# Part buffers, load order and waits in the projection and attention stages of a twelve-sublayer decoder

## The chip, the cores and the metric

The kernel is one program on one core of a Trainium2 chip. The metric is the device time in microseconds (us) of one execution. The core has five engines with instruction streams of their own: PE (TensorE, matmuls), DVE (VectorE), ACT (ScalarE), POOL (GpSimd) and SP (SyncE, which issues most DMAs here). They meet through semaphores.

## The reference, cut to what matters

The reference is a decoder of four levels with three sublayers each (self attention, cross attention to a context of 1024 tokens, and a feed-forward layer), each followed by `x = layernorm(x + sublayer(x))`. Tokens are 4 x 512, channels 256, heads 16 of 16 channels. The parts that the change touches are the projections and the softmax attentions:

```python
q, k, v = x @ Wq.T + bq, y @ Wk.T + bk, y @ Wv.T + bv     # y is x, or the context (4, 1024, 256)
scores = jnp.einsum('bhqd,bhkd->bhqk', q, k) * scale
weights = jax.nn.softmax(scores, axis=-1)
out = jnp.einsum('bhqk,bhkd->bhqd', weights, v)
```

The last cross attention (`L3_xattn`) has no projections: q is x itself, k and v are the context, and a mask of (4, 1, 512, 1024) is added to the scores. The first self attention (`L0_attn`) runs on x and on three coarser samplings of x.

## The kernel before, in words

Twelve sublayers run one behind the other, each as a few stages. Every stage is a block with one instruction stream an engine and semaphores of its own, and the engines meet at its end. Two kinds of stage are changed.

**`project_stage`** (lines 89 to 236) makes q and k and stores them in DRAM as bfloat16 parts. A float32 value is split in three parts (high, middle, low) so that bf16 matmuls can work on it. A unit is a tile of 128 channels by 512 tokens. For a unit of kind `split`, PE multiplies into PSUM (L161), ACT evacuates with the bias to `full` (L194), DVE rounds it to the high part (L224, a CAST) and subtracts to get `rest` (L228), ACT rounds `rest` to the middle part (L172), POOL subtracts to get the low part (L235), and SP stores the parts (L133): two DMAs for a q unit (384 and 256 KB), one for a k unit (384 KB). For a unit of kind `given` (the masked attention alone), the source is in SBUF already: ACT makes the high part straight from it (L183), and DVE, ACT, POOL and SP go on as before. `full` and `rest` have two buffers each, `parts` has three, so a unit's high part waits until the store of the unit three before has landed. On ACT the middle part of a unit stands behind the first step of the unit after it. Units of kind `kept` (values) are evacuated by ACT (L186) behind the split units. There are 32 split units in the pyramid's stage (16 fine, 16 coarse, the coarse ones behind 16 value tiles), 24 in `l1x`, 16 in `l2a`, 16 in `l3a`, and 24 given units in `l3x`, where one DMA brings the whole context (4 MB, `late`, L123) before the first store.

**`attention_stage`** (lines 285 to 914) runs six times: `pyr_coarse`, `pyr_core`, `l1x_core`, `l2a_core`, `l3a_core` (causal) and `l3x_core` (masked). Each has 4 batches of 4 groups of 4 heads, 16 bodies in all. Body g of an engine works on the scores of group g, while the maxima of group g+2 are made between them. The stacks of q and k have four buffers (`RING`), so that SP loads group g+3 in body g. In a body:

- PE: the first scores of group g (L665; they wait for the row of maxima of group g, `row_in`) alternate with the first pass (L597) over group g+2, whose first chunk waits for that group's loads (`loaded`). Behind the first four pairs come the last weighing of group g-1 (L632, `pv_done`) and the transposition of the maxima of group g+1 (`turn`, L611).
- DVE takes the maxima of the first pass (L773, or L769 with the mask) and negates the transposed ones (L787, L790). POOL splits these in three parts (L852, L853, L855, `row_made`).
- SP waits for `pv_done` of group g-1, then loads the values of group g+1 where they come from DRAM (L476; the two pyramid stages), the q and k of group g+3 (L473, 8 DMAs, 9 in `l3a`), and then the row of maxima of group g+1 (L509, 3 DMAs of 4 KB), behind `row_made`:

```python
            def group(b, g):
                before = later(b, g, -1)
                if exists(*before):
                    sync.wait_ge(pv_done, at(*before, nkt, nkt + ahead_tiles))
                    ...
                        load_group(*later(b, g, RING - 1))
                if exists(*later(b, g, 1)):
                    row(*later(b, g, 1))
```

- At the end of the body SP takes its turn with the sums of the weights and their inverses (bodies 0, 1 and 3 of a batch), and in `l3x` with the masks of the next batch.

The 12 bodies from the second to the thirteenth load a group. Loads of `l1x_core` and `l3x_core` have 1024 keys, the others 512. In the masked stage PSUM banks are seeded with `mask_k` by ACT (L715) and DVE (L797, every fourth tile) before the scores are added, and the maxima are taken of scores plus `mask_q`.

## Time and profile before

| | |
|---|---|
| runs | 5061.88, 5063.81, 5067.03 us; median 5063.81 |
| profiled execution | 5061.2 us, span 5059.4 us |
| busy, share of the span | PE 83%, DVE 56%, ACT 47%, POOL 29% |
| mean granted TensorE clock | 0.889 of full |

The stages that the change touches, by the stretches of the trace (us from the span's start; clock as a share of 2.4 GHz):

| stage | stretch | PE busy | clock | DMA share |
|---|---|---|---|---|
| pyramid projections | 17.0 to 138.0 | 106.4 | 0.96 | 0.73 |
| `pyr_coarse` | 136 to 338 | 132.0 | 0.68 | 0.57 |
| `pyr_core` | 338 to 566 | 202.3 | 0.92 | 0.55 |
| `l1x` projections | 1446.0 to 1537.7 | 78.5 | 0.88 | 0.51 |
| `l1x_core` | 1537 to 1958 | 397.2 | 0.94 | 0.32 |
| `l2a` projections | 2318.0 to 2374.5 | 46.6 | 0.89 | 0.50 |
| `l2a_core` | 2374 to 2592 | 203.1 | 0.93 | 0.40 |
| `l3a` projections | 4020.0 to 4079.8 | 49.8 | 0.83 | 0.48 |
| `l3a_core` | 4079 to 4281 | 168.8 | 0.92 | 0.44 |
| `l3x` parts | 4317.5 to 4396.6 | 0 | 0.50 | 0.57 |
| `l3x_core` | 4396 to 4948 | 463.9 | 0.90 | 0.36 |

The profile is one execution. An engine's busy time counts its instructions but not its waits; in the timeline, the brackets behind an instruction give how long the engine stood idle before it and what released it. Since the stages run one behind the other, a microsecond that a stage ends sooner is one off the whole.

### The profile page before, as it was taken

What the parts mean: (1) busy time and instruction counts of PE and PEld (TensorE: products, weight loads), DVE (VectorE), ACT (ScalarE), POOL (GpSimd) and SP (SyncE); (2) the same over time, 40 slices, a digit from 0 to 9 for tenths busy, and PEclk for the clock granted to TensorE, in tenths of its full rate; (3) what the DMA queues carried; (4) which work ended last, traced back from release to release, by engine and by line L of the source; (5) the groups of instructions that cost most, each with busy time, mean ns of one, the idle gap of its engine ahead of it and who ended that gap; (6) DMA issues with size and microseconds to landing.
All of it is one profiled execution on the core that took longest, in us unless ns stands there. A gap on an engine that the chain in (4) does not pass through costs nothing. (4 is left out here: it accounts for less than half of the span.)

```text
span 5059.4 us, 69705 instructions
## 1 busy us (share of the span) xinstructions
PE 4179.5 (83%) x20292; PEld 1977.2 (39%) x20292; DVE 2848.1 (56%) x6426; ACT 2373.1 (47%) x4593; POOL 1483.3 (29%) x1306
## 2 busy tenths in 40 slices
PE   7669766689678996897969799999997988089986
PEld 5322355377443332573334233333335644012223
DVE  3448473501566884004860387878863265298866
ACT  4337431243233775232743354545541245269992
POOL 3111131212130111112220288778880223200111
PEclk9669987799887998897989899999997989579998
DMA  7656212354033332674323311211201144633421
GB/s 249 129 104 120 48 49 34 118 201 147 29 133 56 65 61 64 242 235 126 84 69 148 117 61 60 74 60 59 74 28 45 36 107 86 193 63 90 93 54 37
DMA packets 374291, 486.70 MB, mean 96 GB/s; under 512 B 84772, under 2 KB 288020, under 8 KB 360516
## 3 DMA queue, kind: packets, MB, share of 16 engines
q1 hardware_dynamic: 366528, 447.77, 31.9%
q0 software_dynamic: 6384, 32.61, 2.1%
q8 instruction: 137, 2.24, 0.2%
q10 hardware_dynamic: 1068, 2.66, 0.2%
q14 instruction: 174, 1.43, 0.1%
HBM read 325.07 MB, written 143.92 MB: 93 GB/s over the span
## 5 line engine op out<-in xcount | busy, mean ns | idle before, releaser
L1251 POOL TENSOR_TENSOR lc_totals<-lc_totals,lc_weights 128x1024 f32<-128x1024 f32 (+1 forms) x320 | 623.3, 1948 | 165.1 <-DVE lc_totals L1200 134.1
L1160 ACT ACTIVATE lc_weights<-ps 128x1024 f32<-128x1024 f32 x384 | 393.6, 1025 | 441.0 <-PE ps L1077 430.0
L1181 DVE TENSOR_REDUCE lc_part_max<-ps 128x2 f32<-128x1024 f32 x384 | 466.1, 1214 | 200.5 <-PE ps L1057 199.0
L1077 PE MATMUL ps<-lc_q,lc_k 64*128 64x512 f32 x1536 | 397.3, 596 | 0.0
L1087 PE MATMUL ps<-lc_weights,lc_v 128*64 128x512 f32 x1536 | 372.2, 605 | 0.0
L773 DVE TENSOR_REDUCE l1x_core_part_max<-ps 128x1 f32<-128x512 f32 x512 | 316.4, 681 | 72.5 <-PE ps L597 72.4
L769 DVE CUSTOM_DVE_ANT_0 l3x_core_unused<-ps,l3x_core_mask_q 128x512 f32<-128x512 f32 x512 | 330.7, 686 | 6.4 <-DVE l3x_core_row_max L777 4.9
L732 ACT ACTIVATE l3x_core_weights<-ps 128x512 f32<-128x512 f32 x512 | 327.5, 694 | 7.8 <-PE ps L665 7.3
L732 ACT ACTIVATE l1x_core_weights<-ps 128x512 f32<-128x512 f32 x512 | 266.1, 602 | 84.0 <-PE ps L665 83.8
L715 ACT ACTIVATE ps<-l3x_core_mask_k 128x512 f32<-128x512 f32 x384 | 270.4, 704 | 32.9 <-DMA l3x_core_mask_k<-in_mask_k 32.9
L597 PE MATMUL ps<-l3x_core_k,l3x_core_q 96*128 96x512 bf16 x512 | 214.7, 420 | 54.0 <-DVE l3x_core_part_max L769 38.9
L235 POOL TENSOR_TENSOR proj_parts<-proj_rest,proj_parts 128x512 bf16<-128x512 f32 x112 | 143.9, 1292 | 311.1 <-ACT proj_parts L172 310.7
L597 PE MATMUL ps<-l1x_core_k,l1x_core_q 96*128 96x512 bf16 x512 | 209.0, 411 | 15.7 <-DMA l1x_core_k<-k_parts 11.8
L665 PE MATMUL ps<-l3x_core_q,l3x_core_k 99*128 99x512 bf16 x512 | 198.1, 393 | 19.4 <-ACT ps L715 18.2
L665 PE MATMUL ps<-l1x_core_q,l1x_core_k 99*128 99x512 bf16 x512 | 191.7, 385 | 5.3 <-ACT l1x_core_weights L732 5.3
L1377 DVE SCALAR_TENSOR_TENSOR rn_z<-ps,rn_z 128x256 f32<-128x256 f32 x112 | 45.6, 415 | 258.7 <-PE ps L1348 190.3
L773 DVE TENSOR_REDUCE pyr_core_row_max<-ps 128x1 f32<-128x512 f32 x256 | 158.4, 679 | 53.9 <-PE ps L597 53.8
L1077 PEld LDWEIGHTS ps<-lc_q,lc_k 64*128 64x128 f32 x1536 | 148.0, 189 | 94.0 <-issue 64.9
L773 DVE TENSOR_REDUCE l2a_core_row_max<-ps 128x1 f32<-128x512 f32 x256 | 158.5, 679 | 36.6 <-PE ps L597 36.5
L1057 PE MATMUL ps<-lc_k_round,lc_q_round 64*128 64x512 bf16 x768 | 151.9, 392 | 32.2 <-DVE lc_part_max L1181 20.8
L1087 PEld LDWEIGHTS ps<-lc_weights,lc_v 128*64 128x64 f32 x1536 | 93.3, 136 | 211.1 <-issue 119.4
L732 ACT ACTIVATE pyr_core_weights<-ps 128x512 f32<-128x512 f32 x256 | 133.3, 603 | 77.5 <-PE ps L665 77.4
(477 smaller groups left out, 8558.9 us busy)
## 6 DMA issues: line engine op xcount, KB each, us to landing
cf_w<-in_L1f_w SPq DMA_DIRECT2D x32, 1024.0 KB, 7.2
lc_k<-latent_k SPq DMA_DIRECT2D x32, 768.0 KB, 6.6
lc_v<-latent_values SPq DMA_DIRECT2D x32, 768.0 KB, 5.1
k_parts<-proj_parts SPq DMA_DIRECT2D x56, 384.0 KB, 2.8
latent_k<-feed_staged SPq DMA_DIRECT2D x64, 256.0 KB, 2.3
latent_values<-feed_staged SPq DMA_DIRECT2D x64, 256.0 KB, 2.0
q_parts<-proj_parts SPq DMA_DIRECT2D x40, 384.0 KB, 2.9
q_parts<-proj_parts SPq DMA_DIRECT2D x40, 256.0 KB, 3.0
```

The source lines that it names most:

```text
L597: mm = nc.tensor.matmul(out, q_stack[r][0:rows_a, j, qs], k_stack[r][0:rows_a, j, keys], start=True, stop=not causal)
L665: mm = nc.tensor.matmul(out, k_stack[r][0:rows_b, j, ks], q_stack[r][0:rows_b, j, qs], start=not seeded, stop=not (causal or seeded), skip ...
L715: nc.scalar.activation(k.ps[:, B0 + (g * NS + s) % B_BANKS, 0:nq], seed, ACT.Copy).then_inc(filled, 1)
L732: nc.scalar.activation(weights[:, (g * NS + s) % WEIGHTS, qs], k.ps[:, B0 + (g * NS + s) % B_BANKS, qs], ACT.Exp, scale=scale).then_inc(ex ...
L769: nc.vector.tensor_tensor_reduce(unused[:, n % 2, :], scores, mask_q[:, qi, keys], 1.0, -3.0e38, ALU.add, ALU.max, out).then_inc(a_taken, 1)
L773: nc.vector.reduce_max(out, scores, AX).then_inc(a_taken, 1)
L1057: mm = nc.tensor.matmul(k.ps[:, A0 + j, :], q_round[strip(j), g % 2, qs], k_round[strip(j), g % 2, keys], start=True, stop=True)
L1077: mm = nc.tensor.matmul(out[j], k_tile[g % RING][strip(j), i * P:(i + 1) * P], q_tile[g % RING][strip(j), :], start=False, stop=True)
L1087: mm = nc.tensor.matmul(k.ps[strip(j), ACC, 0:nq], v_tile[g % V_RING][:, i, strip(j)], weights[:, i % TILES, j, :], start=i == 0, stop=i = ...
L1160: nc.scalar.activation(weights[:, i % TILES, :, :], k.ps[:, B0 + (i % 2) * HEADS:B0 + (i % 2 + 1) * HEADS, 0:nq], ACT.Exp, scale=scale).th ...
L1181: nc.vector.reduce_max(own, k.ps[:, A0:A0 + HEADS, :], AX).then_inc(a_taken, 1)
L1251: nc.gpsimd.tensor_tensor(total, total, own, ALU.add).then_inc(added_by_pool, 1)
```

## The change

It has five parts.

1. `project_stage` gets six buffers of parts (`RING = 6`) in place of three.
2. In the masked attention's stage the context comes in eight pieces of 512 tokens (`pieces`), two ahead and one behind each of the first six stores; each given unit waits for its own piece.
3. In `attention_stage` SP sends the row of maxima of group g+1 first in the body, and waits for `pv_done` and issues the loads after it.
4. PE waits for the rows of ones (`set_up`) at the first group's scores and no longer before the first pass, except in the causal stage.
5. At the start of `l3x_core`, SP loads `mask_q` between the first and the second group, and DVE takes the maxima of group 0 and negates them ahead of its first fill.

```diff
-    VALUES = 6
+    VALUES, RING = 6, 6
+    PIECES_AHEAD = 2
...
-        stored_by.append((stored_by[i - 3] if i >= 3 else 0) + 16 * len(units[n][4]))
+        stored_by.append((stored_by[i - RING] if i >= RING else 0) + 16 * len(units[n][4]))
...
-        nc.sbuf_tensor(f"proj_parts_{k.stages}", [P, 3, 3, BANK], BF16) as parts,
+        nc.sbuf_tensor(f"proj_parts_{k.stages}", [P, RING, 3, BANK], BF16) as parts,
...
+            def load_piece(p):
+                if p < len(pieces):
+                    sync.dma_start(pieces[p][0], pieces[p][1]).then_inc(piece_in[p], 16)
+
+            for p in range(PIECES_AHEAD):
+                load_piece(p)
...
-                    for destination, taken in part_stores(unit[4], parts[:, i % 3, :, 0:unit[2]]):
-                        sync.dma_start(destination, taken).then_inc(parts_stored[i % 3], 16)
+                    for destination, taken in part_stores(unit[4], parts[:, i % RING, :, 0:unit[2]]):
+                        sync.dma_start(destination, taken).then_inc(parts_stored[i % RING], 16)
+                    load_piece(PIECES_AHEAD + i)
...
-                    if late and n == late_unit:
-                        act.wait_ge(late_in, 16 * len(late))
-                    if i >= 3:
-                        act.wait_ge(parts_stored[i % 3], stored_by[i - 3])
+                    for p, (_, _, first_unit) in enumerate(pieces):
+                        if first_unit == n:
+                            act.wait_ge(piece_in[p], 16)
+                    if i >= RING:
+                        act.wait_ge(parts_stored[i % RING], stored_by[i - RING])
...
-            for g in range(2):
-                load_group(0, g)
-            if by_batch:
-                load_batch_values(0)
+            load_group(0, 0)
             if mask is not None:
                 for qi in range(nqt):
                     load_mask_q(0, qi)
+            load_group(0, 1)
+            if by_batch:
+                load_batch_values(0)
...
             def group(b, g):
                 before = later(b, g, -1)
+                if exists(*later(b, g, 1)):
+                    row(*later(b, g, 1))
                 if exists(*before):
                     sync.wait_ge(pv_done, at(*before, nkt, nkt + ahead_tiles))
                     if exists(*later(b, g, 1)) and not kept:
                         load_values(*later(b, g, 1))
                     if exists(*later(b, g, RING - 1)):
                         load_group(*later(b, g, RING - 1))
-                if exists(*later(b, g, 1)):
-                    row(*later(b, g, 1))
...
-            if small:
+            if causal:
                 pe.wait_ge(set_up, 16 * n_ones)
...
+                if small and not causal and first(b, g):
+                    pe.wait_ge(set_up, 16 * n_ones)
...
+            maxima(0, 0, range(NCH))
+            negate(0, 0)
             if by_vector:
                 dve.wait_ge(opened, B_BANKS)
                 for s in range(LEAD):
                     if s in by_vector:
                         fill(0, 0, s, 1)
-            maxima(0, 0, range(NCH))
-            negate(0, 0)
             maxima(0, 1, range(NCH))
```

How the instructions move, at three places. On SP in `l2a_core`, from the last initial load on (`q_parts` and `k_parts` are loads of a group, `max_parts` a row of maxima), it stood before as:

```order
L473 DMA l2a_core_k<-k_parts 16x4x512 x3
L509 DMA l2a_core_q<-l2a_core_max_parts 1x16x128 x6
L473 DMA l2a_core_q<-q_parts 48x4x512
L473 DMA l2a_core_q<-q_parts 16x4x512 x3
L473 DMA l2a_core_k<-k_parts 48x4x512
L473 DMA l2a_core_k<-k_parts 16x4x512 x3
L509 DMA l2a_core_q<-l2a_core_max_parts 1x16x128 x3
```

and with the change:

```order
L483 DMA l2a_core_k<-k_parts 16x4x512 x3
L519 DMA l2a_core_q<-l2a_core_max_parts 1x16x128 x9
L483 DMA l2a_core_q<-q_parts 48x4x512
L483 DMA l2a_core_q<-q_parts 16x4x512 x3
L483 DMA l2a_core_k<-k_parts 48x4x512
L483 DMA l2a_core_k<-k_parts 16x4x512 x3
L519 DMA l2a_core_q<-l2a_core_max_parts 1x16x128 x3
```

Two rows (groups 0 and 1) stood ahead of the first load of the loop, and now three do: the row of group 2 is sent before group 4 is loaded. It is the same in all six attention stages.

On SP at the start of `l3x_core`, before:

```order
L473 DMA l3x_core_k<-k_parts 16x4x1024 x3
L473 DMA l3x_core_q<-q_parts 48x4x512
L473 DMA l3x_core_q<-q_parts 16x4x512 x3
L473 DMA l3x_core_k<-k_parts 48x4x1024
L473 DMA l3x_core_k<-k_parts 16x4x1024 x3
L487 DMA l3x_core_batch_values<-in_ctx 128x2048
L480 DMA l3x_core_mask_q<-in_mask_q 128x1024 x4
```

and with the change:

```order
L483 DMA l3x_core_k<-k_parts 16x4x1024 x3
L490 DMA l3x_core_mask_q<-in_mask_q 128x1024 x4
L483 DMA l3x_core_q<-q_parts 48x4x512
L483 DMA l3x_core_q<-q_parts 16x4x512 x3
L483 DMA l3x_core_k<-k_parts 48x4x1024
L483 DMA l3x_core_k<-k_parts 16x4x1024 x3
L497 DMA l3x_core_batch_values<-in_ctx 128x2048
```

The four loads of `mask_q` passed those of the second group and of the values. On DVE, the first fill of a bank (COPY) stood at the head of the stage and now stands behind the 32 chunks of group 0:

```order
L781 ISA l3x_core_unused,l3x_core_part_max<-ps,l3x_core_mask_q 128x512
L781 ISA l3x_core_part_max 128x1
L789 TENSOR_REDUCE l3x_core_row_max<-l3x_core_part_max 128x16
L799 TENSOR_SCALAR l3x_core_max_parts<-ps 16x128
L802 TENSOR_SCALAR l3x_core_negative<-ps 16x128
L809 COPY ps<-l3x_core_mask_k 128x512
L780 MEMSET l3x_core_held_back 1x1
```

So the first maxima no longer stand behind a fill that waits for `mask_k`.

## Rows read from the trace of the kernel before

**Rows 1.** Tile view, one stretch a stage: op, count, duration ns, first and last start

```profile
L611 PE MATMUL ps<-ident,pyr_coarse_row_max x13: 277/382/383, 170.8 to 314.3; 128*16 128x128 f32 x13
...
L611 PE MATMUL ps<-ident,pyr_core_row_max x13: 277/278/278, 385.4 to 535.1; 128*16 128x128 f32 x13
...
L611 PE MATMUL ps<-ident,l2a_core_row_max x13: 277/277/278, 2419.5 to 2560.4; 128*16 128x128 f32 x13
...
L611 PE MATMUL ps<-ident,l3a_core_row_max x13: 276/277/383, 4116.0 to 4254.1; 128*16 128x128 f32 x13
```

**Rows 2.** Waits of `pyr_coarse`: us in total, times, longest

```profile
PE ps L665 <- DMA pyr_coarse_q<-pyr_coarse_max_parts: 53.0, 14, 5.5
```

**Rows 3.** Timeline, PE: first-pass chunk and turn in `pyr_coarse`, `l2a_core`, `l3a_core`

```profile
179.71 0.40 PE L597 MATMUL ps<-pyr_coarse_k,pyr_coarse_q 96*128 96x256 bf16 x1
...
181.90 0.38 PE L611 MATMUL ps<-ident,pyr_coarse_row_max 128*16 128x128 f32 x1
...
2428.50 0.39 PE L597 MATMUL ps<-l2a_core_k,l2a_core_q 96*128 96x512 bf16 x1
...
2431.13 0.28 PE L611 MATMUL ps<-ident,l2a_core_row_max 128*16 128x128 f32 x1
...
4124.46 0.23 PE L597 MATMUL ps<-l3a_core_k,l3a_core_q 99*128 99x128 bf16 x1
...
4126.21 0.28 PE L611 MATMUL ps<-ident,l3a_core_row_max 128*16 128x128 f32 x1
```

**Rows 4.** Timeline, POOL and SP in the body of `l2a_core` that turns at 2419.47

```profile
2421.22 0.42 POOL L855 TENSOR_TENSOR l2a_core_max_parts<-l2a_core_negative,l2a_core_max_parts 16x128 bf16<-16x128 f32 x1
...
2419.59 1.74 SPq L473 DMA_DIRECT2D l2a_core_q<-q_parts  x4
...
2423.28 1.77 SPq L509 DMA_DIRECT2D l2a_core_q<-l2a_core_max_parts  x3
```

**Rows 5.** DMA view, 40 slices of 0.25 us from 171.36, 397.94 and 2419.59

```profile
GB/s 0 0 70 121 195 281 354 377 365 164 148 144 148 172 115 164 164 172 209 176 131 135 127 177 85 51 3 0 0 0 0 0 0 0 0 0 0 0 0 0
...
GB/s 295 262 229 197 262 164 197 37 133 186 227 254 305 307 262 168 152 160 139 152 172 148 160 168 209 197 160 139 139 165 101 33 5 0 0 0 0 0 0 0
...
GB/s 0 0 0 25 139 270 307 234 90 111 164 209 164 246 279 209 221 119 139 130 72 39 14 0 16 1 0 0 0 0 0 0 0 0 0 0 0 0 0 0
```

**Rows 6.** Tile view of `proj_rest`: pyramid's fine units, `l1x`, `l2a`, `l3a`

```profile
L228 DVE TENSOR_TENSOR proj_rest<-proj_full,proj_parts x16: 691/693/1471, 28.1 to 64.7; 128x512 f32<-128x512 f32 x16
...
L228 DVE TENSOR_TENSOR proj_rest<-proj_full,proj_parts x24: 691/693/1471, 1456.2 to 1513.5; 128x512 f32<-128x512 f32 x24
...
L228 DVE TENSOR_TENSOR proj_rest<-proj_full,proj_parts x16: 691/693/1460, 2327.9 to 2364.3; 128x512 f32<-128x512 f32 x16
...
L228 DVE TENSOR_TENSOR proj_rest<-proj_full,proj_parts x16: 691/693/1457, 4029.6 to 4068.7; 128x512 f32<-128x512 f32 x16
```

**Rows 7.** Timeline, DVE and POOL in the `l1x` projections

```profile
1499.80 0.42 DVE L224 CAST proj_parts<-proj_full 128x512 bf16<-128x512 f32 x1
...
1502.41 1.45 DVE L228 TENSOR_TENSOR proj_rest<-proj_full,proj_parts 128x512 f32<-128x512 f32 x1
1505.02 1.03 DVE L224 CAST proj_parts<-proj_full 128x512 bf16<-128x512 f32 x1 [1.15 <-DMA k_parts<-proj_parts]
...
1500.62 2.70 POOL L235 TENSOR_TENSOR proj_parts<-proj_rest,proj_parts 128x512 bf16<-128x512 f32 x2 [1.82 <-ACT proj_parts L172]
```

**Rows 8.** Tile view of `proj_rest`, `l3x` parts

```profile
L172 ACT ACTIVATE proj_parts<-proj_rest x24: 612/613/629, 4318.9 to 4391.1; 128x512 bf16<-128x512 f32 x24
```

**Rows 9.** Stretch view, `l3x` parts: stretch, length, busy PE, PEld, DVE, ACT, POOL, clock, DMA, GB/s

```profile
4317.50:4334.00 16.50, 0.00 (x0) 0.00 (x0) 2.92 (x3) 3.16 (x6) 2.27 (x2) 0.50 0.91 344
```

**Rows 10.** Timeline at the start of `l3x_core`, PE and DVE

```profile
4408.52 1.86 PE L643 MATMUL ps<-l3x_core_q,l3x_core_k 96*128 96x512 bf16 x4 [91.67 <-DMA l3x_core_k<-k_parts]
...
4425.21 0.69 DVE L769 CUSTOM_DVE_ANT_0 l3x_core_unused<-ps,l3x_core_mask_q 128x512 f32<-128x512 f32 x1
```

**Rows 11.** Tile view of `l2a_core_max_parts`: from a row's issue to its landing

```profile
DMA to landing us min/median/max: 1.6/2.1/4.2
```

More of the change, by code:

```diff
@@ L86, in _, with project_stage @@
                 act.dma_start(tile, source).then_inc(loaded, 16)
-def project_stage(k, units, weights, stores=(), late=(), late_unit=0, prefetch=()):
+def project_stage(k, units, weights, stores=(), late=(), late_unit=0, prefetch=(), pieces=()):
     nc = k.nc
@@ L107, in project_stage @@
         nc.sbuf_tensor(f"proj_rest_{k.stages}", [P, 2, BANK], F32) as rest,
-        nc.sbuf_tensor(f"proj_parts_{k.stages}", [P, 3, 3, BANK], BF16) as parts,
+        nc.sbuf_tensor(f"proj_parts_{k.stages}", [P, RING, 3, BANK], BF16) as parts,
         nc.sbuf_tensor(f"proj_value_{k.stages}", [P, VALUES, H, QUAD] if staged else [P, 1, 1, 1], F32) as value,
-        k.stage("weights", "late", "prefetched", "ready", "evacuated", "high", "remainder", "middle", "low", "ones", "parts_stored0",
-                "parts_stored1", "parts_stored2", "others_stored", *(f"value_stored{i}" for i in range(VALUES))) as (
-            weights_in, late_in, prefetched, ready, evacuated, high, remainder, middle, low, ones_set, *stored),
+        k.stage("weights", "late", "prefetched", "ready", "evacuated", "high", "remainder", "middle", "low", "ones",
+                "others_stored", *(f"parts_stored{i}" for i in range(RING)), *(f"value_stored{i}" for i in range(VALUES)),
+                *(f"piece{i}" for i in range(len(pieces)))) as (
+            weights_in, late_in, prefetched, ready, evacuated, high, remainder, middle, low, ones_set, others_stored, *more),
         nc.Block() as block,
     ):
-        parts_stored, others_stored, value_stored = stored[0:3], stored[3], stored[4:]
+        parts_stored, value_stored, piece_in = more[0:RING], more[RING:RING + VALUES], more[RING + VALUES:]
         @block.sync
@@ L141, in _ @@
                 sync.wait_ge(prefetched, 16 * len(prefetch))
-            for r in range(min(3, i)):
-                sync.wait_ge(parts_stored[(i - 1 - r) % 3], stored_by[i - 1 - r])
+            for r in range(min(RING, i)):
+                sync.wait_ge(parts_stored[(i - 1 - r) % RING], stored_by[i - 1 - r])
             if stores:
@@ L171, in take_middle @@
                 act.wait_ge(remainder, i + 1)
-                nc.scalar.activation(parts[:, i % 3, 1, 0:width], rest[:, i % 2, 0:width], ACT.Copy).then_inc(middle, 1)
+                nc.scalar.activation(parts[:, i % RING, 1, 0:width], rest[:, i % 2, 0:width], ACT.Copy).then_inc(middle, 1)
             i = j = 0
@@ L178, in _ @@
                 if unit[0] == "given":
[L179 to L183 removed]
+                    for p, (_, _, first_unit) in enumerate(pieces):
[3 more added lines that the diff above has]
+                        act.wait_ge(parts_stored[i % RING], stored_by[i - RING])
+                    nc.scalar.activation(parts[:, i % RING, 0, 0:unit[2]], unit[1], ACT.Copy).then_inc(high, 1)
                     i += 1
@@ L2738, in masked_attention @@
             project_stage(k, as_is(k.xT, q_parts) + as_is(ctxT, k_parts), [],
-                          late=[(ctxT[:], inp["ctxT"])], late_unit=T // BANK * CH,
+                          pieces=[(ctxT[:, :, t * BANK:(t + 1) * BANK], inp["ctxT"][:, :, t * BANK:(t + 1) * BANK], T // BANK * CH + t * CH)
+                                  for t in range(TC // BANK)],
                           prefetch=[(ow[:], inp["L3x_out_w"]), (ob[:], inp["L3x_out_b"].partition_broadcast(P))])
```

13 lines of the change are left out of this document (6 added, 7 removed).

## The prediction

> **What bounds the kernel now.** I read the stretch view first (its times are in the table above), because the stages stand one behind the other and each must be costed alone. Then the tile view for the pace of the loops, the timeline and the waits for what sets that pace, and the DMA view for when a transfer is through. PE is 83% busy over the span, but the stages that change have other limits. In the four attention stages with 512 keys a body lasts 11.5 to 12.5 us: between the first and the last of 13 turns lie 12 bodies, all of which load a group, so 143.5 / 12 = 11.96 us in `pyr_coarse`, 149.7 / 12 = 12.48 in `pyr_core`, 140.9 / 12 = 11.74 in `l2a_core` and 138.1 / 12 = 11.51 in `l3a_core` [rows 1]. In `pyr_coarse` PE stands 53.0 us waiting for rows of maxima, 14 times [rows 2]; in `l2a_core` it runs through. The split units of the projections follow each other every 2.4 to 2.6 us (57.3 / 23 = 2.49 in `l1x`; 2.44, 2.43 and 2.61 in the others) [rows 6]. The reader is to see there that DVE and POOL take turns: a subtraction of 0.69 us takes 1.45 while POOL's two run, and ends 0.54 us after they do (1502.41 + 1.45 = 1503.86; 1500.62 + 2.70 = 1503.32) [rows 7].
>
> **The row of maxima ahead of the loads.** This is the large term, and I take it for a loss. Body g of SP issues the loads of group g+3, and PE's first pass over that group begins in body g+1, behind the first score. So loads are due about one body after they are issued, as a row is. I follow `l2a_core` from one turn to the next.
> Before: the turn is at 2419.5 [rows 1]. SP issues the loads at once, 2419.59, and is at the row at 2423.28, so 8 loads take 3.7 us to issue and the row 1.77 [rows 4]. Bytes move until slice 22 of the DMA view, 5.5 us after the first issue [rows 5]; a completion comes behind. The pass begins at 2428.50, on loads that have been there for two us, and the next turn is at 2431.13, 2.6 us later [rows 3].
> Now: SP first waits for POOL's last split, which ends at 2421.22 + 0.42 = 2421.64, 2.2 us after the turn [rows 4], issues the row (0.1 + 1.8 us), and then the loads. How long they take from first issue to landing has no row; the bytes are through after 5.5 us in `l2a_core`, and after 6.75 and 8.25 in `pyr_coarse` and `pyr_core`, which load the same sizes [rows 5]. I take 6.5 for `l2a_core` (one us for the completion) and 7.5 for the other two, the middle of their slices; the ends are a us either way. Then the pass waits for the landing, and 2.6 us later comes the turn:
>
> - `l2a_core`: 2.2 + 0.1 + 1.8 + 6.5 + 2.6 = 13.2 us a body, 1.5 more than 11.74: 17.5 us over 12.
> - `pyr_coarse`: its values are issued ahead of the loads (0.45, a quarter of the 1.74 of four loads [rows 4]), and pass to turn takes 181.90 - 179.71 = 2.2 [rows 3]: 2.3 + 1.8 + 0.45 + 7.5 + 2.2 = 14.25, 2.3 more: 27.5 us.
> - `pyr_core`: the same with 2.6, 14.65, 2.2 more: 26 us.
> - `l3a_core`: 9 loads, so 6.8; pass to turn 4126.21 - 4124.46 = 1.75 [rows 3]: 2.3 + 1.8 + 6.8 + 1.75 = 12.65, 1.15 more: 13.7 us.
>
> Sum: **+85 us**, with a us of landing either way +40 to +130. The rows come early and their waits [rows 2] go, but what is late next is the load, by more. SP's own extra turns (sums, inverses, dense copies) stand behind both and fit in the longer body. In `l1x_core` and `l3x_core` a body lasts over 20 us, so a load that is 4 us later is still early: 0.
>
> **Six sets of parts, split units.** The store that a unit waits for is three units further back, so DVE's wait for it (1.15 us before the CAST at 1505.02 [rows 7]) goes. What is next is the turn-taking: CAST 0.42, subtraction 0.69 [rows 7], POOL 1.16 (half of 2.70, less the block at its start), 0.1 between, less 0.15 for each start that is hidden while blocked: 2.05 us a unit. That leaves 23 x 0.44 = 10 us in `l1x`, 15 x 0.38 = 6 in `l2a`, 15 x 0.56 = 8 in `l3a`, 15 x 0.39 = 6 in the pyramid's fine units [rows 6]. A us less each in `l1x`, `l3a` and the pyramid, where the first unit comes slowly from a cold PE or loads fill the queues: 9 + 6 + 7 + 5 = **-27 us**. The value tiles behind are PE's and start that much sooner; the pyramid's coarse units are PE's and only shift. Ends: 0, if the pace is already that of DVE and POOL, and -35.
>
> **The `l3x` parts**, buffers and pieces together. Given units follow every (4391.1 - 4318.9) / 23 = 3.1 us [rows 8]; the middle part of a unit stands on ACT behind the next unit's wait for a store. With six buffers the turn-taking allows 0.69 + 1.16 less 0.3, 1.6 us, 24 units in 38 us. DMA has more to do: 4.2 MB of context, 0.4 of weights, 8 x 0.65 of q and 16 x 0.39 of k are 16.1 MB, at 344 GB/s [rows 9] 47 us. With 3 us at the start and 4 behind the last store: 55 in place of 79.1, **-24 us**; ends -15 and -30. I let the pieces hold no unit up, since a piece is asked for behind each store and the first is needed by unit 8 only.
>
> **The start of `l3x_core`.** PE has group 0 at 4408.52, and DVE begins its maxima at 4425.21, behind a fill that waits for `mask_k` [rows 10]. With `mask_q` right behind group 0, its first quarter (0.5 MB, 1.5 us at 344 GB/s [rows 9]) is there at about 4410, and the fill (0.7) comes later: **-14 us**; ends 0 (the mask lands no sooner) and -16. The first scores wait for DVE's two rounds of maxima, so the gain goes through.
>
> **Rows of ones awaited later**: PE waits for the k loads at the starts, not for these [rows 10], so 0 in five stages and unchanged in the causal one; the loads are the cover, and without them it would be a us at most.
>
> **Sum.** 85 - 27 - 24 - 14 = +20 us on the profiled execution's 5061.2 (span 5059.4, 1.8 around it), which stands 2.6 below the median: 5063.8 + 20 = **5084 us**.
>
> **The rivals.**
> (a) *Loads in time, faster.* A row's DMA lands 2.1 us after its issue [rows 11]; if the last of eight loads did as much, they would be there 3.7 + 2.1 = 5.8 us after the first issue. With the sums above, the bodies would be 12.55, 12.95, 12.5 and 11.65 us (`pyr_coarse`, `pyr_core`, `l2a_core`, `l3a_core`), 0.6, 0.45, 0.75 and 0.15 over today: +23, so 5063.8 + 23 - 65 = 5022 us. It speaks against it that bytes still move after 5.5 to 8.25 us [rows 5]. The sign turns where landings come some 0.4 us sooner than my values (0.4 x 48 bodies = 19). The Trainium skill ("DMA: Bandwidth & Descriptors", "Anatomy of one DMA") has each DMA at some 2.0 us plus its bytes at 436 GB/s. By that rule 0.77 MB would take 3.8 us, a little more than the issues take. By that rule this rival would hold; the DMA view shows 100 to 300 GB/s instead [rows 5]. Chance 0.15.
> (b) *Never late.* PE would be through before SP, and the waits for rows go too: -65 - 53 [rows 2], 4946 us. It needs landings within 5 us. 0.03.
> (c) *The clock falls.* Stalls of 2 to 3 us in every body make PE run at 1.2 GHz, as in `pyr_coarse`, where the transposition takes 382 ns and not 277 [rows 1]. Then pass to turn doubles in `pyr_core` (+2.6 x 12 = 31) and `l3a_core` (+1.75 x 12 = 21): 5136 us. For it: one transposition of `l3a_core` at 383 [rows 1]; against: `pyr_core` has gaps today and all its 13 turns take 277 or 278 ns. 0.12.
> (d) *Six buffers buy nothing for split units*, as DVE and POOL set the pace: 5084 + 27 = 5111 us. 0.1.
>
> **How the numbers follow.** My forecast has 0.6, the rivals 0.4. The range is 5040 to 5135: it holds the forecast with its landings some 0.8 us off, (d) and the edge of (c), and leaves out (a) and (b). About 0.2% (10 us) is what a measurement of this kernel can tell from no change. Faster: (a), (b) and a tail of the forecast, 0.2. Same: the part of the forecast with +/-10 us, 0.14. Slower: 0.66.
>
> **What would show it.** Right: turns 13 to 15 us apart in the four short stages; PE's waits at first-pass chunks for `q_parts` or `k_parts`, none for rows of maxima; `l3x` parts near 55 us; DVE's first maxima of `l3x_core` some 14 us after its loads begin; split units every 2.05 us. Wrong: bodies of 12 us or less with PE waiting for nothing (a), transpositions at 382 ns in `pyr_core` (c), split units at 2.4 (d).

## The result, and the profile after

| | before | after |
|---|---|---|
| median | 5065.17 us (4 runs, 5061.88 to 5067.03) | 5127.95 us (4 runs, 5120.47 to 5131.85) |
| ratio, 95% interval | | 1.0117 [1.0105, 1.0130] |
| profiled span | 5059.4 us | 5130.1 us |
| mean granted clock | 0.889 | 0.883 |

The changed kernel is 63 us slower. The forecast had been 5084, in a range of 5040 to 5135: the direction and the mechanism are as forecast, and the loss is three times the forecast one. By its number alone the result is nearer to rival (c), the falling clock, at 5136.

Where it went, from PE's first and last instruction of each stage in the two profiled executions ("parts" is what lies between the stages, their only changed piece being the projections):

| stretch | before | after | difference | forecast |
|---|---|---|---|---|
| start to `pyr_coarse` (pyramid parts) | 146.1 | 136.3 | -9.8 | -5 |
| `pyr_coarse` | 190.7 | 222.3 | +31.6 | +27.5 |
| `pyr_core` | 217.6 | 264.6 | +47.0 | +26 |
| to `l1x_core` (parts) | 983.6 | 971.9 | -11.7 | -9 |
| `l1x_core` | 407.8 | 408.8 | +1.0 | 0 |
| to `l2a_core` (parts) | 425.5 | 422.1 | -3.4 | -6 |
| `l2a_core` | 208.4 | 239.3 | +30.9 | +17.5 |
| to `l3a_core` (parts) | 1498.4 | 1489.5 | -8.9 | -7 |
| `l3a_core` | 190.6 | 216.8 | +26.2 | +13.7 |
| to `l3x_core` (parts) | 129.1 | 107.7 | -21.4 | -24 |
| `l3x_core` | 538.6 | 526.1 | -12.5 | -14 |

The four short stages lost 135.7 us where 85 were forecast; all the other rows together gained 66.7 where 65 were forecast (the space between the two pyramid stages grew by 1.2). So the whole miss lies in one term.

**The pace.** The turns of the four short stages in the kernel after, as in [rows 1]:

```profile
L621 PE MATMUL ps<-ident,pyr_coarse_row_max x13: 278/382/383, 160.2 to 335.7; 128*16 128x128 f32 x13
...
L621 PE MATMUL ps<-ident,pyr_core_row_max x13: 277/382/383, 408.0 to 604.7; 128*16 128x128 f32 x13
...
L621 PE MATMUL ps<-ident,l2a_core_row_max x13: 277/278/383, 2474.3 to 2647.2; 128*16 128x128 f32 x13
...
L621 PE MATMUL ps<-ident,l3a_core_row_max x13: 277/382/383, 4193.6 to 4357.8; 128*16 128x128 f32 x13
```

A body now lasts 175.5 / 12 = 14.62, 16.39, 14.41 and 13.68 us. The median of a turn has gone from 278 to 382 ns in `pyr_core` and from 277 to 382 in `l3a_core`: more than half of them stand in stretches at the lower clock, which before was so in `pyr_coarse` only.

**What PE waits for.** Waits of PE in the kernel after (us in total, times, longest), in place of [rows 2]:

```profile
PE ps L607 <- DMA pyr_coarse_k<-k_coarse: 85.5, 13, 12.2
...
PE ps L607 <- DMA pyr_core_k<-k_parts: 51.0, 13, 12.0
...
PE ps L607 <- DMA l3a_core_k<-in_slopes: 29.6, 12, 3.5
PE ps L607 <- DMA l2a_core_k<-k_parts: 29.4, 13, 8.1
...
PE ps L677 <- DMA pyr_coarse_q<-pyr_coarse_max_parts: 9.5, 6, 4.8
```

L607 is the first pass (L597 before). Each of its waits comes once in a body that loads, and once at a stage's start (the longest, 8 to 12 us; `l3a`'s start is booked under the rows of ones). The rows of maxima, 53 us of waits in `pyr_coarse` before, are down to 9.5. One late transfer has been traded for another one, as the prediction says.

**One body.** The timeline of SP, POOL and PE in the body of `l2a_core` that turns at 2474.29, against [rows 3, 4]:

```profile
2474.29 0.28 PE L621 MATMUL ps<-ident,l2a_core_row_max 128*16 128x128 f32 x1
...
2476.05 0.42 POOL L867 TENSOR_TENSOR l2a_core_max_parts<-l2a_core_negative,l2a_core_max_parts 16x128 bf16<-16x128 f32 x1
...
2476.49 1.77 SPq L519 DMA_DIRECT2D l2a_core_q<-l2a_core_max_parts  x3
...
2478.30 2.00 SPq L483 DMA_DIRECT2D l2a_core_q<-q_parts  x4
...
2480.35 1.85 SPq L483 DMA_DIRECT2D l2a_core_k<-k_parts  x4
...
2484.96 0.39 PE L607 MATMUL ps<-l2a_core_k,l2a_core_q 96*128 96x512 bf16 x1 [1.63 <-DMA l2a_core_k<-k_parts]
...
2487.58 0.28 PE L621 MATMUL ps<-ident,l2a_core_row_max 128*16 128x128 f32 x1
```

Turn to row 2.2, row 1.8, first load to pass 6.66, pass to turn 2.62: 13.29 us, where the prediction had 13.2 by the same steps. This is a body at the high clock. The other kind, in `pyr_core`:

```profile
425.61 0.28 PE L621 MATMUL ps<-ident,pyr_core_row_max 128*16 128x128 f32 x1
...
427.99 1.78 SPq L519 DMA_DIRECT2D pyr_core_q<-pyr_core_max_parts  x3
...
430.45 1.92 SPq L483 DMA_DIRECT2D pyr_core_q<-q_parts  x4
...
437.88 0.39 PE L607 MATMUL ps<-pyr_core_k,pyr_core_q 96*128 96x512 bf16 x1 [3.24 <-DMA pyr_core_k<-k_parts]
...
438.10 0.38 PE L677 MATMUL ps<-pyr_core_q,pyr_core_k 99*128 99x512 bf16 x1
...
439.03 0.63 PE L677 MATMUL ps<-pyr_core_q,pyr_core_k 99*128 99x512 bf16 x1
...
440.02 1.94 PE L642 MATMUL ps<-pyr_core_weights,pyr_core_v 128*32 128x512 f32 x8
...
441.89 0.38 PE L621 MATMUL ps<-ident,pyr_core_row_max 128*16 128x128 f32 x1
```

The first chunk follows a wait of 3.24 us and still takes 0.39. From 439.03 on the same matmuls take 0.63 and the weighing 1.94 (1.06 ahead of the wait), and pass to turn is 4.01 us, not 2.6. The clock falls behind the gap, over the very stretch that everything then waits for. The stretch view (columns as in [rows 9]) has the granted clock at 1.00 up to 438, through the wait, and then at:

```profile
438.00:440.00 2.00, 2.00 (x7) 0.61 (x6) 1.70 (x3) 1.38 (x3) 0.00 (x0) 0.73 0.04 8
440.00:442.00 2.00, 2.00 (x10) 0.32 (x10) 0.82 (x2) 0.30 (x1) 0.00 (x0) 0.50 0.00 0
```

The body before this one has the same: a wait of 4.09 us, and matmuls of 0.63 us from 0.8 us behind it on. Not every wait has it: behind two of the twelve in `pyr_core`, of 2.70 and 2.79 us, pass to turn stays at 2.62.

**The parts.** The tile view of `proj_rest` after (pyramid's fine units, `l1x`, `l2a`, `l3a`, and the middle parts of `l3x`), against [rows 6, 8]:

```profile
L238 DVE TENSOR_TENSOR proj_rest<-proj_full,proj_parts x16: 691/694/1457, 27.9 to 56.9; 128x512 f32<-128x512 f32 x16
...
L238 DVE TENSOR_TENSOR proj_rest<-proj_full,proj_parts x24: 691/694/1457, 1526.7 to 1573.5; 128x512 f32<-128x512 f32 x24
...
L238 DVE TENSOR_TENSOR proj_rest<-proj_full,proj_parts x16: 691/694/1459, 2390.4 to 2421.2; 128x512 f32<-128x512 f32 x16
...
L238 DVE TENSOR_TENSOR proj_rest<-proj_full,proj_parts x16: 692/694/1457, 4117.6 to 4148.4; 128x512 f32<-128x512 f32 x16
...
L181 ACT ACTIVATE proj_parts<-proj_rest x24: 612/614/631, 4426.0 to 4473.8; 128x512 bf16<-128x512 f32 x24
```

The split units come every 1.93, 2.03, 2.05 and 2.05 us (46.8 / 23 = 2.03), where 2.05 was forecast from the turns that DVE and POOL take. The given units of `l3x` come every 47.8 / 23 = 2.08 us, down from 3.1. That is a mean of two paces. At both ends of the stage they come every 1.8 us, and between 4437.5 and 4452.7 every 3.05. There the DMA engines are full (share 1.07), and ACT waits for a store ahead of each of seven units, 12.0 us in all:

```profile
4440.00:4450.00 10.00, 0.00 (x0) 0.00 (x0) 2.42 (x4) 4.32 (x8) 3.62 (x3) 0.50 1.07 393
...
4442.94 0.63 ACT L193 ACTIVATE proj_parts<-l3x_ctxT 128x512 bf16<-128x512 f32 x1 [2.00 <-DMA q_parts<-proj_parts]
```

**The start of `l3x_core`.** PE's first matmul and DVE's first maximum, against [rows 10]:

```profile
4491.36 1.89 PE L653 MATMUL ps<-l3x_core_q,l3x_core_k 96*128 96x512 bf16 x4 [67.50 <-DMA l3x_core_k<-k_parts]
...
4493.88 0.69 DVE L781 CUSTOM_DVE_ANT_0 l3x_core_unused<-ps,l3x_core_mask_q 128x512 f32<-128x512 f32 x1
```

2.5 us from one to the other in place of 16.7 (4425.21 - 4408.52), 14.2 less. The first load of the stage is issued at 4479.46, so the maxima begin 14.4 us behind it, as the prediction has it.

### The profile page after: what moved, and what is told of

The parts are those of the page before. It is cut to its first block and busy times, and to the rows that moved or that the text cites. A ratio compares the mean times of both kernels' runs of the same rounds, so it can differ in the third digit from the quotient of the medians.

```text
span 5130.1 us, 69704 instructions
## 1 busy us (share of the span) xinstructions
PE 4215.5 (82%) x20292; PEld 1981.6 (39%) x20292; DVE 2872.0 (56%) x6426; ACT 2380.2 (46%) x4593; POOL 1491.2 (29%) x1306
## 5 line engine op out<-in xcount | busy, mean ns | idle before, releaser
L607 PE MATMUL ps<-l3x_core_k,l3x_core_q 96*128 96x512 bf16 x512 | 215.5, 422 | 39.7 <-DVE l3x_core_part_max L781 25.1
L607 PE MATMUL ps<-l1x_core_k,l1x_core_q 96*128 96x512 bf16 x512 | 209.6, 412 | 15.7 <-DMA l1x_core_k<-k_parts 11.8
L1389 DVE SCALAR_TENSOR_TENSOR rn_z<-ps,rn_z 128x256 f32<-128x256 f32 x112 | 45.9, 417 | 261.1 <-PE ps L1360 236.9
L744 ACT ACTIVATE pyr_core_weights<-ps 128x512 f32<-128x512 f32 x256 | 135.7, 602 | 111.8 <-PE ps L677 111.3
```

The costliest lines, as they stand in the source:

```text
L607: mm = nc.tensor.matmul(out, q_stack[r][0:rows_a, j, qs], k_stack[r][0:rows_a, j, keys], start=True, stop=not causal)
L744: nc.scalar.activation(weights[:, (g * NS + s) % WEIGHTS, qs], k.ps[:, B0 + (g * NS + s) % B_BANKS, qs], ACT.Exp, scale=scale).then_inc(ex ...
```

## The experiments

Each has its own runs of the kernel before on the same chip; ratios are to those. L-numbers of the changed kernel hold for the experiments made from it, moved by up to six lines where one adds lines.

### Undo the order on SP

```diff
                 before = later(b, g, -1)
-                if exists(*later(b, g, 1)):
-                    row(*later(b, g, 1))
                 if exists(*before):
...
                         load_group(*later(b, g, RING - 1))
+                if exists(*later(b, g, 1)):
+                    row(*later(b, g, 1))
```

> The change with the old order on SP (loads of a group, then the row of maxima); the other four parts stay. Theory (the order alone makes the loss): outside the four short stages the changed kernel is 65 us ahead of the one before, and inside them it lost some 136 us of its span; with the old order the four stages are back at bodies of 11.5 to 12.5 us and the time is 5065 - 65 = 5000 us, ratio 0.987. Rival (the loss comes from the stores or loads that now crowd the queues, or from the later wait for the rows of ones): the bodies stay near 14 to 16 us and the time stays above 5060.

Measured: 4991.33 us, ratio 0.9857 [0.9840, 0.9873]. The four stages last 188.8, 220.2, 210.1 and 187.9 us, within 3 us of before the change, and every other stretch stays within 4 us of the kernel after. Its turns in `pyr_core` and `l3a_core`:

```profile
L621 PE MATMUL ps<-ident,pyr_core_row_max x13: 277/278/383, 373.8 to 526.6; 128*16 128x128 f32 x13
...
L621 PE MATMUL ps<-ident,l3a_core_row_max x13: 277/278/382, 4084.3 to 4220.8; 128*16 128x128 f32 x13
```

12.73 and 11.38 us a body, at the higher clock again but for one turn in each. The order alone makes the loss: 5128 - 4991 = 137 us (132 by the ratios).

### The order on SP alone

The kernel before, with the same few lines moved the other way.

> The kernel before with only the new order on SP. Theory: the four short stages lose what they lost in the changed kernel, 136 us in the span of one execution, and nothing else moves: 5065 + 128 (the medians' +63, and 65 that the other parts gave) = 5190 to 5200 us, ratio 1.025; l1x_core and l3x_core within 2 us of before. Rival (the new order hurts only together with the other parts): under 5100.

Measured: 5202.67 us, ratio 1.0269 [1.0247, 1.0290], 3 us above what was expected. PE's waits are those of the kernel after:

```profile
PE ps L597 <- DMA pyr_coarse_k<-k_coarse: 86.2, 13, 12.7
...
PE ps L597 <- DMA pyr_core_k<-k_parts: 50.0, 13, 11.4
...
PE ps L597 <- DMA l3a_core_k<-in_slopes: 32.8, 12, 3.8
```

`l1x_core` lasts 407.8 us and `l3x_core` 538.1, as before. So the edit costs 139 us on the kernel before (5202.67 - 5064.15, its own runs of before; 136 by the ratio) and 137 us on the change, and the two sides add up: +137 to +139 for the order, -73 for the rest (4991.33 - 5064.15), +63 for both.

### Three and four sets of parts

Both with the loads first, as in the first experiment.

```diff
-    VALUES, RING = 6, 6
+    VALUES, RING = 6, 3
```

> The change with the old order on SP and three sets of parts instead of six; pieces and the rest stay. Theory (the wait for the store of three units before was the pace): split units go back from 2.05 us to 2.4 to 2.6 us each, and the l3x parts from 58 us to some 75: 27 + 15 more than the same kernel with six sets, 5040 us. Rival (the pieces alone mend the l3x parts): l3x parts near 60 us, 5027.

Measured: 5048.91 us, ratio 0.9968 [0.9958, 0.9978], so the three sets more are worth 58 us (5048.91 - 4991.33) of the 73, more than the 42 expected. By stretches of the profiled executions it is 8.4 us in the pyramid (136.5 to 144.9 until `pyr_coarse`), 14 in `l1x`, 6 in `l2a`, 2 in `l3a` and 20 in `l3x`, 50 in all; the profiled execution with three sets was the fastest of its nine, 9 us below their median. Here the units of `l1x` and the middle parts of `l3x` come every 2.53 and 2.93 us:

```profile
L238 DVE TENSOR_TENSOR proj_rest<-proj_full,proj_parts x24: 691/693/1469, 1458.6 to 1516.8; 128x512 f32<-128x512 f32 x24
...
L181 ACT ACTIVATE proj_parts<-proj_rest x24: 612/613/630, 4316.1 to 4383.5; 128x512 bf16<-128x512 f32 x24
```

> The change with the old order on SP and four sets of parts, between the three of before and the six of the change. Theory (the store of three units before was late by little: with three sets a unit took 2.5 us in place of 2.05, so it asks for 3 x 0.45 = 1.4 us more of room, and one set more gives 2.05): split units every 2.05 to 2.1 us, the time within 5 us of six sets, 4991 to 4996. Rival (the stores' own time sets the pace in stretches, and each set more takes a third of the loss away): 5010 to 5030.

With `RING = 4` in that line, measured: 4990.11 us, ratio 0.9870 [0.9853, 0.9888], the same as with six. In `l1x` the pace is that of six sets, in `l3x` it is 51.0 / 23 = 2.22 us, where the first experiment has 46.9 / 23 = 2.04:

```profile
L238 DVE TENSOR_TENSOR proj_rest<-proj_full,proj_parts x24: 691/694/1459, 1447.6 to 1494.5; 128x512 f32<-128x512 f32 x24
...
L181 ACT ACTIVATE proj_parts<-proj_rest x24: 613/615/632, 4279.2 to 4330.2; 128x512 bf16<-128x512 f32 x24
```

One set more does nearly all of it. The store was late by less than one unit.

### The context in one piece

With the loads first and six sets; the `pieces` list has one entry, the whole of `ctxT`, awaited by the first unit of the context.

```diff
-                          pieces=[(ctxT[:, :, t * BANK:(t + 1) * BANK], inp["ctxT"][:, :, t * BANK:(t + 1) * BANK], T // BANK * CH + t * CH)
-                                  for t in range(TC // BANK)],
+                          pieces=[(ctxT[:], inp["ctxT"], T // BANK * CH)],
```

> The change with the old order on SP and the whole context in one DMA of 4 MB at the start, six sets of parts. Theory (DMA volume bounds the l3x parts, and the pieces only spread it): the first stores wait behind the 4 MB, and the stage takes 3 to 8 us longer than with pieces; 5000 to 5008 us. Rival (the pieces were the main gain there): the stage is back at 70 to 79 us, 5015 or more.

Measured: 4989.75 us, ratio 0.9852 [0.9836, 0.9869], with 4991 for pieces: nothing. The middle parts take 45.9 us here, and 46.9 in the first experiment:

```profile
L181 ACT ACTIVATE proj_parts<-proj_rest x24: 612/613/630, 4295.1 to 4341.0; 128x512 bf16<-128x512 f32 x24
```

The stage and what surrounds it is 107.5 us against 106.6. The expected 3 to 8 us of loss are a miss. Both kernels have the DMA engines full for 25 to 30 us of the stage (share 0.96 to 1.08), so it may be that the bytes must be moved either way and their order makes no difference; beyond this pair no run shows it.

### The old start of `l3x_core`

With the loads first; `mask_q` goes behind group 1 and the values, and DVE's fill ahead of the maxima of group 0, as before.

> The change with the old order on SP, and l3x_core started as before (mask_q behind group 1 and the values, the fill ahead of the maxima of group 0). Theory: the stage's first turn is again some 41 us after its first matmul instead of 28, 14 us more than with the new start: 5014 us. Rival (the first scores wait for something else, and the gain is given back later): 5000 to 5005.

Measured: 5002.22 us, ratio 0.9882 [0.9867, 0.9897], 11 us more than with the new start (13 by the ratios). `l3x_core` lasts 540.9 us against 525.3, 15.6 more, and its first turn comes 42.3 us after its first matmul against 27.8. DVE's start shows the wait:

```profile
4369.21 0.69 DVE L809 COPY ps<-l3x_core_mask_k 128x512 f32<-128x512 f32 x1 [34.78 <-DMA l3x_core_mask_k<-in_mask_k]
4369.82 0.69 DVE L781 CUSTOM_DVE_ANT_0 l3x_core_unused<-ps,l3x_core_mask_q 128x512 f32<-128x512 f32 x1
```

So the gain at the new start is still there at the stage's end: 14 us at its head, 11 to 13 by the times, 15.6 by the stage. The total lies in the rival's 5000 to 5005 only because the expectation counted from 5000 and the first experiment measured 4991.

### Rows of ones awaited early

With the loads first; the wait for `set_up` stands ahead of the first pass in all six stages.

> The change with the old order on SP and the rows of ones awaited ahead of the first pass again, in all stages. Theory (the k loads land after the rows of ones at every start): first turns 5.1, 10.4, 20.1, 10.4, 7.4 and 27.8 us after the first matmul as with the change, the first matmul of each stage no later, 4991 us within 5. Rival (the ones were late where few loads stand ahead): the first matmuls come 1 to 2 us later in some stages, up to 5000.

Measured: 4983.14 us, ratio 0.9856 [0.9839, 0.9873], the same ratio as with the late wait (the time is 8 us less than there, and its own runs of before 7 us less). The first turns are at the same distances (5.1, 10.4, 20.1, 10.4, 7.4, 27.8 us). No stretch between two stages is more than 0.2 us longer either. The loads are the cover.

### The row first in the long stages alone

```diff
+                if nk > BANK and exists(*later(b, g, 1)):
+                    row(*later(b, g, 1))
                 if exists(*before):
...
+                if nk <= BANK and exists(*later(b, g, 1)):
+                    row(*later(b, g, 1))
```

> The change with the new order on SP only in the stages with 1024 keys (l1x_core, l3x_core) and the old one in the other four. Theory (a body of over 20 us has room for both orders, so neither is worth anything there): the same as the old order everywhere, 5000 us within 5. Rival (the row sent first is worth something where the loads have time): 5 to 20 us less.

Measured: 4986.59 us, ratio 0.9860 [0.9845, 0.9875], the same as the old order everywhere, whose own ratio is 0.9857 (the 5 to 20 us of the rival were counted from 5000, not from the 4991 measured). `l1x_core` lasts 407.8 us, `l3x_core` 523.3. Here the rows go out 2.3 us after the turn in place of 4.1 to 4.2, which is worth nothing, as no one waits for them.

### Extra matmuls in the gap

The changed kernel, with matmuls that compute nothing needed, on the group loaded before, into the bank that the first chunk overwrites. The wait for that bank (`a_taken`) moves ahead of them.

```diff
                     if n == 0:
+                        if nk <= BANK and not first(b, g, 2):
+                            o = (r - 1) % RING
+                            for _ in range(FILLERS):
+                                nc.tensor.matmul(k.ps[:, A0 + (g * NCH) % A_BANKS, 0:wide], q_stack[o][0:rows_a, j, 0:P],
+                                                 k_stack[o][0:rows_a, j, :], start=True, stop=True)
                         pe.wait_ge(loaded[r], loads_done(b, g))
```

> The changed kernel as it is, with four extra matmuls (128x512, on the group loaded before) into the free bank ahead of each wait for a group's loads, in the stages with 512 keys. They do no useful work; they fill a part of the gap in which PE waits. Theory (some 50 of the 136 us lost are the lower clock that the gaps bring: turns at 382 ns in pyr_core, l2a_core and l3a_core): turns are at 277 ns in l2a_core and most of pyr_core, bodies 13.2 to 15.0 us there, and the time is 5128 - 30 = 5100 us or less. Rival (the clock only follows and costs nothing, as the landing of the loads sets the pace): within 10 us of 5128, or slower by what the extra matmuls take.

Measured with `FILLERS = 4`: 5101.21 us, ratio 1.0085 [1.0070, 1.0101]. That is 27 us less than the changed kernel (16 by the ratios; the four stages are 21.6 shorter in the profiled executions), with 56 x 4 matmuls more. Its turns in `pyr_core` and `l2a_core`:

```profile
L627 PE MATMUL ps<-ident,pyr_core_row_max x13: 277/278/383, 411.5 to 600.0; 128*16 128x128 f32 x13
...
L627 PE MATMUL ps<-ident,l2a_core_row_max x13: 276/277/277, 2466.9 to 2628.4; 128*16 128x128 f32 x13
```

`l2a_core` has no turn at the lower clock left, 13.46 us a body; the prediction's steps give 13.2. `pyr_core` has 15.71, with a few turns at 383 ns, outside the expected 15.0. `l3a_core` has 13.11, with its pass to turn at 2.08 us in place of 2.45. The expectation's 50 us for the clock is more than this run gives back.

> The kernel with fillers (four extra matmuls ahead of each wait for loads), with eight of them in pyr_core, where PE still waited 2.0 us at each first pass with four, and 3.4 us passed from the first pass to the turn in place of 2.6. Theory (what is left over in pyr_core is the clock too): eight extra matmuls of 0.4 us fill the 3.2 us of the wait, from pass to turn takes 2.6 to 2.8 us there, the body 14.9 in place of 15.7, and the time is 9 us less than 5101: 5092. Rival (in pyr_core something else than the clock stretches the first pass, the loads of values for one): pass to turn stays at 3.4 and the time at 5101 or above.

Measured with eight in `pyr_core`: 5107.43 us, ratio 1.0084 [1.0063, 1.0104]. In `pyr_core` it is as expected: 178.7 / 12 = 14.89 us a body, and the stage is 7.2 us shorter (249.9 against 257.1).

```profile
L627 PE MATMUL ps<-ident,pyr_core_row_max x13: 277/278/382, 414.9 to 593.6; 128*16 128x128 f32 x13
```

The total isn't: the forecast 5092 was missed by 15 us. In this profiled execution `l2a_core` and `l3a_core`, whose code is the same in both, lasted 4.2 and 4.8 us longer, and why is open. The two totals can't be told apart; the stage can.

### The loads ahead of the row, and sooner

In all kernels so far SP issues the loads behind the last weighing of group g-1. They need only the scores of group g-1 to be through, and these are once the last but one weighing is.

```diff
                 before = later(b, g, -1)
+                if exists(*before) and small and exists(*later(b, g, RING - 1)):
+                    sync.wait_ge(pv_done, at(*before, nkt, nkt + ahead_tiles - 1))
+                    load_group(*later(b, g, RING - 1))
                 if exists(*later(b, g, 1)):
                     row(*later(b, g, 1))
-                if exists(*before):
+                if exists(*before) and not (small and (kept or by_batch)):
                     sync.wait_ge(pv_done, at(*before, nkt, nkt + ahead_tiles))
...
                         load_values(*later(b, g, 1))
-                    if exists(*later(b, g, RING - 1)):
+                    if not small and exists(*later(b, g, RING - 1)):
                         load_group(*later(b, g, RING - 1))
```

> The change, but the loads of group g+3 are issued ahead of the row, behind the last-but-one weighing of group g-1 (at the end of the body before) and no longer behind the last one, some 4 us sooner than in any kernel so far; the row follows, then the values. Theory (what a body needs is loads a body ahead and a row soon after it is made, and SP's turn behind the last weighing made one of them late): SP is free when a row is made, so rows go out 1.6 us sooner in l2a_core and 3 us sooner in pyr_coarse than before, and loads are never late: pyr_coarse gives back most of its 53 us of waits for rows, l3a_core and pyr_core some: 5000 - 50 = 4950 us. Rival (rows are bound by the DMA's own latency, or other limits come next): within 10 us of the kernel with the old order.

Measured: 4955.64 us, ratio 0.9790 [0.9777, 0.9803], the fastest of all kernels here, 2.1% under the kernel before and 36 us under the change with its old order. SP in a body of `l2a_core`:

```profile
2376.90 1.74 SPq L483 DMA_DIRECT2D l2a_core_q<-q_parts  x4
...
2378.69 1.85 SPq L483 DMA_DIRECT2D l2a_core_k<-k_parts  x4
...
2379.80 0.28 PE L624 MATMUL ps<-ident,l2a_core_row_max 128*16 128x128 f32 x1
...
2382.19 1.77 SPq L519 DMA_DIRECT2D l2a_core_q<-l2a_core_max_parts  x3
```

The loads start 2.9 us ahead of the turn and are issued at 2380.54, and SP stands ready when POOL has made the row, which goes out 2.39 us after the turn, as soon as in the changed kernel. The gain is where a row was late: `pyr_coarse` lasts 173.8 us against 188.8, `pyr_core` 208.3 against 220.2, `l3a_core` 178.8 against 187.9; `l2a_core`, where none was late, lasts 207.0, as in three of the other kernels with the loads first. The total is as expected, `pyr_coarse` is not: it was to give back most of its waits for rows, and four fifths remain.

```profile
PE ps L680 <- DMA pyr_coarse_q<-pyr_coarse_max_parts: 42.6, 13, 8.1
```

Its rows go out 0.9 us sooner on average than in the kernel before (4.3 us after the turn for 5.1), not 3. More than half of what remains, 22.4 us, is in three bodies in which SP is held by its own turns with inverses and dense copies and then issues the loads first. In one of them POOL had made the row at 227.67:

```profile
223.94 6.39 SPq L553 DMA_DIRECT2D pyr_dense_coarse<-pyr_att_coarse  x8
...
234.96 1.85 SPq L519 DMA_DIRECT2D pyr_coarse_q<-pyr_coarse_max_parts  x3
...
238.21 0.39 PE L680 MATMUL ps<-pyr_coarse_q,pyr_coarse_k 99*128 99x256 bf16 x1 [7.96 <-DMA pyr_coarse_q<-pyr_coarse_max_parts]
```

## Why the prediction was right, and where it was short

**The row ahead of the loads: right in kind and place, some 50 us too small.** Loads were late in every loading body of the four short stages and in no other, PE waited for them at the first pass, and the two experiments on the order show that this edit alone costs 137 to 139 us. The steps of a body, as means over its twelve loading bodies in the kernel after, beside what the prediction had:

| stage | turn to first load | first load to landing | landing to pass | pass to turn | body | forecast |
|---|---|---|---|---|---|---|
| `pyr_coarse` | 5.01 (4.55) | 7.31 (7.5) | 0.12 (0) | 2.19 (2.2) | 14.62 | 14.25 |
| `pyr_core` | 5.13 (4.55) | 7.26 (7.5) | 0.12 (0) | 3.89 (2.6) | 16.39 | 14.65 |
| `l2a_core` | 4.42 (4.1) | 6.56 (6.5) | 0.12 (0) | 3.31 (2.6) | 14.41 | 13.2 |
| `l3a_core` | 4.45 (4.1) | 6.67 (6.8) | 0.12 (0) | 2.45 (1.75) | 13.68 | 12.65 |

The landing, which the prediction held for its uncertain term and gave a microsecond either way, was right within 0.3 us, and what it lacks makes up for the 0.12 us from landing to pass, which was left out. Two other terms were not:

- *Pass to turn* was taken from [rows 3] as fixed: "the pass waits for the landing, and 2.6 us later comes the turn". It is 1.29, 0.71 and 0.70 us longer in three stages, 2.7 x 12 = 32 us. The body of `pyr_core` above shows how, and the extra matmuls show that it is the clock: they shorten pass to turn to 2.62 in `l2a_core` (four of them) and 2.71 in `pyr_core` (eight), the values of the high clock. In `l3a_core` they give back only about half of it (2.08 with four); its turns at 382 ns say the same, but no run has it at the high clock throughout. The Trainium skill ("Perfetto Trace Analysis", "Matmul Optimizations") has advice on this: matmuls should run back to back in batches, since the matmul engine scales its power with its use. The trace agrees (0.38 against 0.63 us for the same matmul).
- *Turn to first load* was 0.3 to 0.6 us longer, 1.7 x 12 = 20 us. The prediction put the row's issue right behind POOL and the loads right behind the row. SP has some 0.1 to 0.3 us between each two of its steps, the values take 0.6 us and not 0.45 (the DMA at 429.81 in `pyr_core`), and in a few bodies the issue itself is slower.

**The rivals.** (c), the clock falls, had 0.12 as a case of its own, in which every body runs at 1.2 GHz. It happened in a part of the bodies: (c) has 2.6 us a body in `pyr_core`, 1.75 in `l3a_core` and nothing in `l2a_core`; measured are 1.29, 0.70 and 0.71. By the prediction's own list, turns at 382 ns in `pyr_core` were the sign of (c), and the bodies of `pyr_core`, at 16.4 us, are outside its 13 to 15. The argument against it, that `pyr_core` has gaps in the kernel before and no turn at 382, was weak: those were six waits of 9.3 us in total, the longest 2.3, and the new ones are a mean of (51.0 - 12.0) / 12 = 3.25 us in every body. A better prediction would have put part of (c) in the forecast: a stage gets gaps of the length that `pyr_coarse` had, so price it with the pace of `pyr_coarse` between the two clocks. (a) and (b) fell: the loads land 6.6 to 7.3 us after their first issue, not 5.8. The rule of the Trainium skill ("DMA: Bandwidth & Descriptors", "Anatomy of one DMA") gives an estimate of 3.8 us for these bytes, by which they would have been in time. The page gives it per DMA and for those that POOL issues, and the trace of these eight from SP doesn't agree (6.6 to 7.3 us). (d) fell: split units come every 2.03 to 2.05 us.

**The range.** 5128 is inside 5040 to 5135, but near its edge and not for the main reason that the range was made wide. That width was for the landing, which used none of it; the clock and the issue used it. That the number is inside is in that part luck.

**Six sets, split units: right.** 2.05 us forecast, 2.03 to 2.05 measured outside the pyramid, 1.93 within. -27 forecast; -9.8, -11.7, -3.4 and -8.9 make -34. The first to the last subtraction of each stage is 7.6, 10.5, 5.6 and 8.3 us shorter, 32 in all; the -3.4 of `l2a` is low by what else lies in that stretch, as it is 417.9 to 418.9 us long in all nine experiments with the change and four or six sets, not 422.1. The same step from three sets back to six is worth 30 us there in the third experiment. That four sets do as well as six was not asked by the prediction, and it could have been: the wait of 1.15 us in [rows 7] is less than one unit.

**The `l3x` parts: right.** 55 us forecast; the space that holds the stretch fell by 21.4, which from 79.1 makes 57.7. The buffers do it, 20 us; the pieces, which the prediction put together with them, nothing. Units come every 2.0 to 2.1 us there, not the 1.6 that the forecast allowed to the engines. That fits its other term, 47 us of DMA for 24 units: the trace has 1.8 us a unit where the engines set the pace, and 3.05 while the DMA engines are full.

**The start of `l3x_core`: right**, 14 us forecast, 14.2 at DVE's first maximum, 12.5 to 15.6 by the stage's length and 11 to 13 by the times of the two kernels. **Rows of ones: right**, 0.

**The sum.** +136 - 34 - 21 - 12.5 + 1 (`l1x_core`) + 1.2 (between the pyramid stages) = +70.7 of the spans, +63 of the medians.

## What to carry to other kernels

When a transfer is moved behind another on a queue, look at who needs it next and by when: here a load had 2.1 us of room in a body of `l2a_core` and 1 us in the pyramid's, and was moved back by 4, while what it made way for, the row, had cost PE 53.0 us in `pyr_coarse`, 14.3 in `l3a_core`, 9.3 in `pyr_core` and 0.3 in `l2a_core`. Ask first if the thing that stands in the way can start earlier; its true condition (the scores are through) was met some 3 us ahead of the one that the code waited for (the weighing is through), and using it made both the loads and most of the rows early: 36 us. Then see what else the queue does: SP's own turns made the latest rows that were left. And a gap that is put into a matmul loop costs its own length and then some of the clock in the stretch behind it: price the work behind a new gap at both clocks (here 2.6 and 3.3 to 3.9 us from pass to turn).

## What the runs showed of the hardware

- A wait of 3.24 us of PE was followed, before the next turn, by a fall of the clock from 2.4 to 1.2 GHz: 512-column bf16 matmuls went from 0.38 to 0.63 us and the weighing from 1.06 to 1.94, while ahead of the wait they ran at full rate (granted clock 1.00 up to the end of the wait, 0.50 from 2 us behind it). With the gap cut from 3.25 to 1.12 us a body by matmuls that nobody needed, `pyr_core` was 14.7 us shorter (264.6 to 249.9), at much the same landing times (7.26 and 7.11 us from the first issue).
- Eight loads, 0.77 MB in all, are not slowed by a row that goes ahead of them: they land 7.31 and 6.56 us after their first issue in `pyr_coarse` and `l2a_core`, and 7.61 and 6.56 with the loads first, where two bodies of `pyr_coarse` have 9.4 and 9.6. The row is what gains: it lands 3.2 and 3.1 us after its first issue ahead of the loads, and 4.3 and 3.3 us behind them in these two stages.
- DVE and POOL take turns at the split units: of the 24 subtractions of DVE in `l1x`, about half take 1.46 us in place of 0.69, and each of these begins while one of POOL's runs. This pace, 2.05 us a unit, stands once the stores are out of the way.
